# Attention scores in 32x64 column tiles, a reversed second token tile, last products per expert, and a new order of calls, in a fused attention and expert block

## The reference

```
xn = layernorm(x)
out = x + attn(xn) + ffn(xn)

attn: q, k, v = split(xn @ w_qkv.T);  att = softmax(q k.T / sqrt(128))
      y = einsum('bqk,bvd->bqd', att, v) @ w_fc.T + b_fc    # k and v sum apart
      layernorm(xn + y) * gamma + beta
ffn:  h = rms(xn);  16 heads of 8:  q = rms(h wq), k = rms(h wk), v = h wv
      a = softmax(causal(q k.T / sqrt(8))) v;  x1 = xn + (a @ wo.T, first 32 columns 0)
      xf = rms(x1);  weights = top 2 of 4 of softmax(xf @ gate.T), normalised
      moe = w0 o0 + w1 o1 + w2 o2 + w3 o3   # o0: one gelu, o1: silu gate, o2: three gelus, o3: two
      x1 + (moe, first 32 columns 0)
```

## Time and profile before

| | |
|---|---|
| median of three runs | 224.91 us |
| the profiled execution | 224.7 us |
| its span | 223.0 us |
| TensorE busy | 203.4 us (91%) |
| ScalarE busy | 167.6 us (75%) |
| VectorE busy | 137.7 us (62%) |
| GpSimd busy | 106.7 us (48%) |
| granted TensorE clock, mean | 0.991 |

### The profile page before, as it was taken

The page is one execution under the profiler, slowest core; times in us unless marked ns, Lnnn a source line. Parts: engine busy times, 40 slices in busy tenths (PEclk is TensorE's granted clock), DMA queues, the critical chain, the costliest instruction groups (busy, mean ns, idle before and its releaser), DMA issues.

```text
span 223.0 us, 6031 instructions
## 1 busy us (share of the span) xinstructions
PE 203.4 (91%) x2158; PEld 149.8 (67%) x2158; DVE 137.7 (62%) x529; ACT 167.6 (75%) x287; POOL 106.7 (48%) x190
## 2 busy tenths in 40 slices
PE   7888689999999999999999787999999999999872
PEld 6655455568787678676888464578776887678661
DVE  4389938769563526598992476393587555637604
ACT  6457867899999997956689846779789997944530
POOL 7974788973831153147722369425630168010330
PEclk9999999999999999999999999699999999999999
DMA  5950000000000000000000000000000000000001
GB/s 152 296 188 3 3 0 4 0 3 1 0 3 26 0 3 26 0 0 6 0 25 3 26 0 3 1 3 1 3 24 3 1 3 24 3 0 3 24 1 31
DMA packets 5393, 5.00 MB, mean 22 GB/s; under 512 B 498, under 2 KB 4850, under 8 KB 5362
## 3 DMA queue, kind: packets, MB, share of 16 engines
q1 hardware_dynamic: 5216, 4.59, 6.6%
q10 hardware_dynamic: 146, 0.00, 0.0%
HBM read 3.54 MB, written 1.05 MB: 21 GB/s over the span
## 4 chain that ended last, share of the span: by engine, by line
PE 50%; ACT 16%; issue 12%; DVE 12%; POOL 8%; POOLq 0%; ACTq 0%; DVEq 0%
PE even_ps L366 7%; PE scores_ps L252 6%; PE odd_ps L339 5%; PE even_ps L339 5%; PE a_ps L277 5%; ACT probs L742 4%; PE even_ps L398 4%; PE odd_ps L398 3%; PE odd_ps L382 3%; PE odd_ps L192 3%; PE a_ps L222 3%; POOL probs L574 2%; ACT L796 2%; DVE acc L1247 2%; PE a_ps L281 2%
## 5 line engine op out<-in xcount | busy, mean ns | idle before, releaser
L574 POOL TENSOR_SCALAR_AFFINE_SELECT probs<-probs 128x1024 f32<-128x1024 f32 x32 | 35.0, 1094 | 48.6 <-ACT probs L742 48.4
L742 ACT ACTIVATE probs<-scores_ps 128x1536 f32<-128x1536 f32 x32 | 46.4, 1451 | 12.8 <-PE scores_ps L252 12.4
L252 PE MATMUL scores_ps<-qT,kT 32*128 32x128 f32 (+1 forms) x512 | 29.9, 347 | 2.9 <-ACT probs L742 2.7
L252 PEld LDWEIGHTS scores_ps<-qT,kT 32*128 32x128 f32 x512 | 23.5, 184 | 11.9 <-issue 9.5
L366 PE MATMUL even_ps<-l_h,mid 128*128 128x256 f32 x128 | 30.7, 383 | 0.2 <-DVE e_s L1041 0.2
L366 PEld LDWEIGHTS even_ps<-l_h,mid 128*128 128x128 f32 x128 | 23.8, 190 | 4.6 <-ACT l_h L796 0.9
L339 PE MATMUL odd_ps<-xfT,up 128*128 128x256 f32 x80 | 22.9, 401 | 0.8 <-ACT u_h L796 0.8
L277 PE MATMUL a_ps<-probs,v_aug 128*32 128x256 f32 x256 | 20.7, 395 | 1.9 <-ACT kT L848 0.5
L796 ACT ACTIVATE l_h<-even_ps 128x512 f32<-128x512 f32 x24 | 14.3, 597 | 10.0 <-PE even_ps L366 8.3
L796 ACT ACT_TABLE_LOAD x16 | 20.5, 1283 | 1.0 <-PE odd_ps L339 0.3
L1247 DVE SCALAR_TENSOR_TENSOR acc<-even_ps,wts,acc 128x96 f32<-128x96 f32 x32 | 10.1, 317 | 17.4 <-issue 9.9
(11 more groups left out here) (151 smaller groups left out, 435.0 us busy)
## 6 DMA issues: line engine op xcount, KB each, us to landing
x_sb<-in_x SPq DMA_DIRECT2D x8, 128.0 KB, 5.5
out<-acc SPq DMA_DIRECT2D x8, 128.0 KB, 1.8
mid<-in_mid SPq DMA_DIRECT2D x1, 640.0 KB, 7.4
up<-in_up SPq DMA_DIRECT2D x1, 578.0 KB, 6.4
downs<-in_down SPq DMA_DIRECT2D x1, 512.0 KB, 8.3
first<-in_first SPq DMA_DIRECT2D x1, 320.0 KB, 3.9
proj<-in_proj SPq DMA_DIRECT2D x1, 192.0 KB, 2.8
row<-in_rows SPq DMA_DIRECT2D x1, 192.0 KB, 4.8
```

The source lines that it names most:

```text
L252: ins = T.matmul(ps, kT[p][rows, g, kt * P:(kt + 1) * P], qT[p][rows, kt * P:SEQ], start=kt == 0, stop=kt == 1 and not searching, tile_pos ...
L574: nc.gpsimd.affine_select(out=own, in_=own, compare_op=ALU.is_ge, fill=0.0, base=0, pattern=[[0, LANES * TILES], [1, P]], channel_multipli ...
L742: nc.scalar.activation(probs[g][:, :, 0:SEQ + P], scores_ps[:, :, 0:SEQ + P], ACT.Exp).then_inc(s["exp_done"], 1)
```

## The change

- `scores`: all groups but the first use array tiles of 32 rows by 64 columns, so a group has 16 matmuls. Tokens of the second tile are stored in reversed order (the input and the output are turned outside of the kernel). Then the first 64 keys of the first tile are needed by all 256 queries, the next 64 by the last 192; of the second tile's keys the first 64 are needed by 64 queries and the next 64 by 128. What is left out keeps old numbers, which the mask sets to 0.
- `mask`: two selections over 128x512 a group, with opposite signs, in place of one.
- The last batch's `down` becomes four calls `last_down(e)`, one for an expert, in the order 0, 1, 3, 2, that write to `scores_ps`; each waits for its own hidden layer alone. VectorE adds each product when it is there, and each token tile is stored by itself.
- Every engine's list of calls has a new order. TensorE's changes the form of its array tiles 124 times instead of 135 (in the branch that runs), ScalarE's holds 26 table loads instead of 34, and 8 calls of `keep_busy`'s matmul are left of 13.

```diff
+HIDDEN_FILL = ("E0", "E1B", "L3", "U3")
+LAST_ORDER = (0, 1, 3, 2)
...
+                whole = searching or (n == 0 and g == 0)
                 for kt in range(TILES):
-                    for lane in range(LANES):
-                        rows = slice(32 * lane, 32 * lane + 32)
-                        ps = scores_ps[:, lane, 0:SEQ] if kt == 0 else scores_ps[:, lane, SEQ:SEQ + P]
-                        ins = T.matmul(ps, kT[p][rows, g, kt * P:(kt + 1) * P], qT[p][rows, kt * P:SEQ],
-                                       start=kt == 0, stop=kt == 1 and not searching, tile_position=(32 * lane, 0))
+                    for half in range(1 if whole else 2):
+                        part = slice(0, P) if whole else COLUMN_TILES[half]
+                        keys = slice(kt * P + part.start, kt * P + part.stop)
+                        seen = slice(part.start, SEQ) if kt == 0 else slice(P, P + part.stop)
+                        at_col = (SEQ if kt else part.start) if not whole else kt * SEQ
+                        for lane in range(LANES):
+                            rows = slice(32 * lane, 32 * lane + 32)
+                            ins = T.matmul(scores_ps[part, lane, at_col:at_col + seen.stop - seen.start],
+                                           kT[p][rows, g, keys], qT[p][rows, seen], start=kt == 0,
+                                           stop=kt == 1 and not searching, tile_position=(32 * lane, part.start))
...
+            def last_down(e):
+
+                n = BATCHES - 1
+                pe.wait_ge(s["exp_done"], GROUPS * BATCHES)
+                pe.wait_ge(read_sem(HIDDEN_FILL[e]), at[HIDDEN_FILL[e], n] + 1)
+                for j in range(TILES):
+                    for ci in range(HC):
+                        for rows in COLUMN_TILES:
+                            tokens = slice(j * P + rows.start, j * P + rows.stop)
+                            ins = T.matmul(scores_ps[rows, e, j * KEPT:(j + 1) * KEPT], hidden[e][n % 2][:, ci, tokens],
+                                           downs[:, e, ci, MASKED:], start=(ci == 0), stop=(ci == HC - 1),
+                                           tile_position=(0, rows.start))
+                ins.then_inc(s["last_full"], 1)
...
-                keep_busy(4); fold_weights(); x_turn(0); keep_busy(1); qkv_project(0, 0); x_turn(1); qkv_project(0, 1)
...
-                e3_up_layer(7); fc_row(7); l1_layer(7); e1_second(7); l2_layer(7); e0_up(7); l3_layer(7); down(7, 0)
-                down(7, 1)
+                keep_busy(1); x_turn(0); keep_busy(1); qkv_project(0, 0); fold_weights(); x_turn(1); qkv_project(0, 1)
...
+                l2_layer(7); e1_second(7); l3_layer(7); e3_up_layer(7); last_down(0); last_down(1); last_down(3)
+                last_down(2)
...
+            def store_last():
+                for j in range(TILES):
+                    sp.wait_ge(s["last_summed"], j + 1)
+                    sp.dma_start(rows_of(out, BATCHES - 1)[:, j, :], acc[BATCHES - 1][:, j, :]).then_inc(s["out_done"], 16)
...
             def mask(n, g):
 
                 pool.wait_ge(s["exp_done"], GROUPS * n + g + 1)
-                own = probs[g][:].rearrange("p l (n q) -> p (l n) q", q=SEQ)[:, :, 0:P]
-                nc.gpsimd.affine_select(out=own, in_=own, compare_op=ALU.is_ge, fill=0.0, base=0,
-                                        pattern=[[0, LANES * TILES], [1, P]], channel_multiplier=-1
-                                        ).then_inc(s["masked"], 1)
+                for kt, sign in enumerate((1, -1)):
+                    own = probs[g][:, :, kt * SEQ:kt * SEQ + P]
+                    ins = nc.gpsimd.affine_select(out=own, in_=own, compare_op=ALU.is_ge, fill=0.0, base=0,
+                                                  pattern=[[0, LANES], [sign, P]], channel_multiplier=-sign)
+                ins.then_inc(s["masked"], 1)
...
-            search_constants(); ln_variance(0); ln_pow(0); h_square(0); ln_variance(1); h_mean(0); ln_pow(1); h_eps(0)
-            h_square(1); h_pow(0); x1_start(0); h_mean(1); x1_start(1); h_eps(1); biased(0); h_pow(1); biased(1)
...
+            ln_variance(0); ln_pow(0); h_square(0); h_mean(0); h_eps(0); h_pow(0); ln_variance(1); ln_pow(1)
+            h_square(1); h_mean(1); biased(0); x1_start(0); h_eps(1); biased(1); h_pow(1); search_constants()
...
+            def last_down(j, e):
+
+                n, place = BATCHES - 1, LAST_ORDER.index(e)
+                dve.wait_ge(s["last_full"], place + 1)
+                if place == 0:
+                    dve.wait_ge(s["acc_ready"], n + 1)
+                    need("weights", n)
+                else:
+                    need(("last", j, LAST_ORDER[place - 1]), n)
+                kept = acc[n][:, j, MASKED:]
+                ins = V.scalar_tensor_tensor(out=kept, in0=scores_ps[:, e, j * KEPT:(j + 1) * KEPT],
+                                             scalar=wts[n % 2][:, j, e:e + 1], in1=kept, op0=ALU.mult, op1=ALU.add)
+                if place < EXPERTS - 1:
+                    then(ins, ("last", j, e), n)
+                else:
+                    ins.then_inc(s["last_summed"], 1)
...
+    def second_tile_turned(a):
+        tiles = _np.asarray(a).reshape(-1, 2, P, P)
+        return _np.stack([tiles[:, 0], tiles[:, 1, ::-1]], axis=1).reshape(-1, 2 * P, P)
...
-        "x": inputs["L0_attn_x"],
+        "x": second_tile_turned(inputs["L0_attn_x"]),
```

More of the change, by code:

```diff
@@ L261, in scores @@
                     for lane in range(LANES):
-                        own = scores_ps[:, lane, :].rearrange("p (n q) -> p n q", q=SEQ)[:, :, 0:P]
-                        ins = T.matmul(own, ident_bf[:], later_keys[:].unsqueeze(1).to_broadcast([P, TILES, P]),
-                                       start=False, stop=True)
+                        for kt, later in enumerate((later_keys, later_keys_q)):
+                            ins = T.matmul(scores_ps[:, lane, kt * SEQ:kt * SEQ + P], ident_bf[:], later[:], start=False,
+                                           stop=kt == TILES - 1)
                 ins.then_inc(s["scores_full"], 1)
@@ L389, in down @@
                 ps = claim(fill, n)
-                for done in ("E0", "E1B", "L3", "U3"):
+                for done in HIDDEN_FILL:
                     pe.wait_ge(read_sem(done), at[done, n] + 1)
@@ new lines, in batches @@
+                weigh_v(2, 0); gate(1); down(0, 0); down(0, 1); scores(2, 3); q0_project(3); l1_layer(1)
+                weigh_v(2, 1); e0_up(1); a0_scores(3, 0); l2_layer(1); e3_in(1); weigh_v(2, 2); weigh_v(2, 3)
+                e1_first(1); qk_turn(3); e1_second(1); wo_project(2); find_maxima(3); scores(3, 0); l3_layer(1)
+                e3_up_layer(1); a0_scores(3, 1); qkv_project(4, 0); scores(3, 1); down(1, 0); down(1, 1); xf_turn(2)
+                scores(3, 2); gate(2); l1_layer(2); fc_row(3); e3_in(2); scores(3, 3); weigh_v(3, 0); weigh_v(3, 1)
@@ new lines, in batches @@
+                l2_layer(2); e0_up(2); x_turn(5); weigh_v(3, 2); weigh_v(3, 3); e1_first(2); e1_second(2)
+                qkv_project(4, 1); wo_project(3); l3_layer(2); e3_up_layer(2); qkv_project(5, 0); q0_project(4)
+                down(2, 0); down(2, 1); xf_turn(3); qkv_project(5, 1); l1_layer(3); qk_turn(4); e3_in(3); e1_first(3)
+                e3_up_layer(3); gate(3); find_maxima(4); scores(4, 0); e1_second(3); l2_layer(3); e0_up(3)
+                scores(4, 1); qk_turn(5); l3_layer(3); a0_scores(4, 0); down(3, 0); down(3, 1); scores(4, 2)
@@ new lines, in batches @@
+                e3_up_layer(4); e1_first(4); gate(4); qk_turn(6); e1_second(4); xf_turn(5); l3_layer(4); e3_in(5)
+                a0_scores(6, 0); find_maxima(6); scores(6, 0); down(4, 0); gate(5); down(4, 1); scores(6, 1)
+                a0_scores(6, 1); qk_turn(7); e1_first(5); scores(6, 2); e3_up_layer(5); fc_row(6); l1_layer(5)
+                q0_project(7); scores(6, 3); a0_scores(7, 0); weigh_v(6, 0); weigh_v(6, 1); a0_scores(7, 1)
+                find_maxima(7); scores(7, 0); weigh_v(6, 2); weigh_v(6, 3); l2_layer(5); e1_second(5); wo_project(6)
@@ new lines, in batches @@
+                scores(7, 1); fc_row(7); l3_layer(5); weigh_v(7, 0); e0_up(5); xf_turn(6); scores(7, 2); weigh_v(7, 1)
+                down(5, 0); down(5, 1); scores(7, 3); gate(6); l1_layer(6); weigh_v(7, 2); e3_in(6); weigh_v(7, 3)
+                e1_first(6); e0_up(6); wo_project(7); l2_layer(6); e3_up_layer(6); l3_layer(6); xf_turn(7)
+                e1_second(6); l1_layer(7); e3_in(7); gate(7); down(6, 0); down(6, 1); e1_first(7); e0_up(7)
+                l2_layer(7); e1_second(7); l3_layer(7); e3_up_layer(7); last_down(0); last_down(1); last_down(3)
@@ L1345, in batches @@
[L1345 to L1349 removed]
+                ln_normalise(0); ln_statistics(1); ln_moments(1); scale_projection(); ln_normalise(1); head_scales()
```

304 lines of the change are left out of this document (142 added, 162 removed).

## The result

The changed kernel takes **214.49 us**, the median of four runs (213.70 to 216.29), against 224.55 (223.94 to 224.93) for the kernel before on the same chip: a ratio of 0.9566 with a 95% interval from 0.9497 to 0.9634, 10.1 us faster. The profiled execution is the longest of the four: it took 216.29 us with a span of 214.1. Two of the others kept TensorE's granted clock at 1.0 throughout and took 213.70 and 214.04 us; why this one didn't is part of what follows. Runs over 1.5% above the fastest of their kernel are left out of the ratios, which concerns three of the twelve runs of one experiment (e10).

The account below looks back on a forecast made before the run. TensorE's calls were taken to bound 140 of 223 us, chains of waits the rest. Scores -4.8, forms -1.4, masks +0.6, start -2.5, middle -1.0, end -1.9 sum to -11.0: 224.7 to 213.7 us, range 207 to 221.5.

Parts of the forecast that it names:

- scores: 31 of 32 score groups: each 0.706 us instead of 0.86 through column halves running side by side, 4.8 us less.
- masks: GpSimd's two selections a group instead of one: 0.6 us more, from three places where TensorE waits for a mask.
- start: Start of the kernel: earlier root and shorter VectorE chain 3.2 us, less 0.7 for fewer dummies: 2.5 us less.
- end: Batch 7's down products cover the last gelu and two products follow instead of four: 1.9 us less.
- forms, tables, middle: Fewer array-form changes 1.4 us less, fewer ScalarE table loads nothing, shorter wait and clock drop mid-kernel 1.0 less.
- I count all 31: Scores: the full 0.154 us saving counted in each of 31 groups, 4.8 us, even where TensorE isn't the bound.
- a half waits for the other half's pass: Rival for the score groups: matmuls start in written order, 384 columns as now, 1.5 us saved, 217.0 us; chance 0.17.
- The root at 4.0 us: Start, GpSimd: with mask constants moved behind both batches' roots, the first root starts at about 4.0 us, 1.9 earlier.
- the first xn at 4.8: Sign at the start: batch 0's xn, which follows the first root, at 4.8 us; 6.71 before.
- The first scores about 3 us before now: Sign at the start: the first score group begins about 3 us earlier than in the kernel before.
- A granted clock under 1.0 in the first 40 us: Sign that the prediction would be wrong: TensorE's granted clock below 1.0 in the first 40 us.
- I took a third of 3.1: Middle: of TensorE's 1.30 us wait behind batch 5's scores and 1.8 us of lowered clock, 1.0 us comes back.

Follow-up runs that it names:

- e10: Kernel before with the mask constants moved behind the roots of batches 0 and 1 in GpSimd's order: ratio 1.0093, 2.1 us slower.
- e1: Changed kernel with every score group on whole 32x128 tiles again: 217.3 us, ratio 0.9664.
- e2: Kernel before with only the new score tiles, reversed second tile and two masks; old orders and old end: 222.75 us, ratio 0.9936.
- e6: Kernel before with its one mask a group split into two of 128x512: 224.01 us, ratio 0.9987.
- e5: Changed kernel with the old end (two calls of down products, eight products on VectorE, one store): 216.51 us, ratio 0.964.
- e8: Changed kernel unaltered, run again for its own spread: 214.05 us, ratio 0.9532.
- e3: Changed kernel without the reversal of the second token tile, halves streaming 384 and 256 columns: 214.83 us, ratio 0.9581.
- e9: e4 with four more dummy matmuls where TensorE waits for batch 0's normalised heads: 214.19 us, ratio 0.9532.
- e7: Changed kernel with more dummy matmuls at the start, ahead of the first turn and of batch 1's projection: 214.88 us, ratio 0.9577.
- e11: e9 with two added dummy matmuls instead of four: 213.87 us, ratio 0.9534.
- e4: Changed kernel with batch 1's root moved ahead of the biased copies and the residual's start in GpSimd's order: 215.22 us, ratio 0.9567.

## Why the prediction was right, and where its steps were not

213.7 us were predicted and 214.49 measured. The score group got shorter by the mechanism named; that the total fits so well is in part luck, since the terms were not all of the right size:

| term | predicted | measured | by |
|---|---|---|---|
| scores | -4.8 | -2.2 to -3.0 in the new order (-2.3 by the traces), -1.4 in the old | e1, e2 |
| masks | +0.6 | -0.9 to +0.3, in the old order | e6 |
| start | -2.5 | -1.6, -2.2 or -3.8 (first scores) | profiles of the changed kernel, e5, e8 |
| end | -1.9 | -1.6 by the traces, -2.5 by the medians | e5, e8 |
| forms, tables, middle | -2.4 | not separated | |

**Scores.** The group came out nearly as worked out (0.706, read 0.70 in the chain; by its hold on TensorE, 0.865 and 0.729, it gained 0.136 us and not 0.154), and e3 shows the reason, two queues of which the longer counts. What was mis-sized is the sentence "I count all 31". A group's gain is a gain only until the next call that waits for another engine. From 40 to 120 and 140 to 200 us I had called TensorE the bound on account of its busy share, but there ScalarE's gelus and VectorE's products finish only just ahead of the calls that need them, and 0.136 us is more than that margin at some of them: of 4.2 us about 1.9 were given back. The Trainium skill (TensorE: Matmul & The Clock Gate, "The mechanism") has matmuls in strict program order; if that meant that a half waits for the other half's pass, e3 and the changed kernel would have had equal groups. They have 0.81 and 0.70, and matmuls of 128 columns start ahead of those of 64 that are written before them, so the measurement decides.

**The start.** The root at 4.0 us (4.08) and the first xn at 4.8 (4.83) came as said. "The first scores about 3 us before now" came as 1.57 in one profile and 3.81 in the other; of the ends that I gave, 0.8 and 3.2, the first lies inside and the second outside. I hadn't seen that GpSimd's new order puts two copies that need the rows ahead of batch 1's root, so that the start follows the landing of a transfer. "A granted clock under 1.0 in the first 40 us" was named as a sign of being wrong; it happened, behind that wait. That the fewer dummies bring it is not shown: e8 and e9 have as few of them ahead of the first turn, and no drop in their profiles. But the fewer dummies are not without a price: in e5's profile, with the same calls at the start, TensorE's calls still run at half speed up to about 10.7 us, and the first scores come at 18.20 us with no drop behind them, 1.6 us later than in e8, where I had taken 0.7. e10 shows that the term's 1.9 us for the earlier root was no property of that edit: alone it costs 2.1 us. In the new TensorE order batch 2 isn't needed so early; what the move is worth there no run shows alone, only that the first scores come 1.6 to 3.8 us sooner with all changes of the start together.

**The middle.** The wait of the earlier trace rows is 0.59 us instead of 1.30:

```profile
138.23 0.41 PE L189 MATMUL b_ps<-ident,xf 128*128 128x128 f32 x2 [0.59 <-DVE xf L1241]
```

The stage's idle time fell by 1.21 us, no wait of over 2 us came ahead of batch 4's second norm, and the clock stayed up. What the drop had cost is 1.2 us, not 1.8, and only in some runs: of 58 runs of the kernel before beside the experiments, 27 with a clock of 0.994 or more took 223.61 to 224.20 us and 31 with 0.992 or less 224.65 to 225.72 us, 223.9 and 225.1 in the mean; in both profiles with such a clock (before and e6) it is this drop. Nor does the wait alone bring the drop: e2's profile, in the old order, has it and keeps a clock of 1.00 over the 6 us behind.

```profile
139.56 0.44 PE L189 MATMUL b_ps<-ident,xf 128*128 128x128 f32 x2 [1.32 <-ACT a_exp L777]
```

I took a third of 3.1; the rows speak for more, but no run has this part alone.

**Forms and tables.** ScalarE is 9.6 us less busy, as said. Whether any of that came back, and what the 11 fewer changes of form gave, wasn't tried. By subtraction from the first pair of profiles, 8.9 us of span less 2.3 for the scores, 1.6 for the start and 1.6 for the end leaves 3.4 us for forms, tables, masks and the middle, 1.8 predicted; this is a remainder, and the drop that only the kernel before has in the middle of this pair is in it.

**The end.** The four calls had no wait; e5 has one of 0.86 us and four products behind the last matmul, 1.6 us in all.

So the total was right by two errors of opposite sign: about 2 us too much for the scores and, by that remainder, 1.6 too little for forms, tables, masks and the middle.

## What to carry to other kernels

A shorter call pays only up to the margin of the next wait: multiply the saving by the calls, then look, call by call, at how long the partner engine's result had been ready, not at the busy share. A move in one engine's order has no price of its own (here 2.1 us lost in one order, and no delay seen in the other); ask which call of the others stands first behind the place where it lands. And where a kernel's time varies with something at its start, compare a stretch behind the cause (here from the first exponential on), which agreed to 0.05 us in five profiles with the same calls there (190.58 to 190.63 us; the first, e7, e8, e9 and e11) whose spans differ by 2.3.

## What the runs showed of the hardware

- In two-pass f32 matmuls on 32x64 tiles the two column halves of a strip run beside each other. With 384 columns in the longest, the group held TensorE for 0.809 us, with 320 for 0.729; on 32x128 tiles with 384 it was 0.865. 64 columns fewer gave 0.080 us, 1.25 ns each, less than the 1.68 that I had used.
- One and the same kernel ran with and without a drop of the clock to its lower level in its first 20 us. The drops seen there stand behind TensorE's waits of 1.85 us (changed kernel), 1.93 (e1) and 1.57 (e4); the profiles without one had waits of 1.26 us (e5) or less ahead of the first scores, and with e4's wait filled by dummies all eleven runs had a clock of 0.997 to 1.0. But a wait doesn't settle it: in the middle of the old order the clock fell behind a wait of 1.30 us (before) and kept its level behind one of 1.32 (e2).
- When TensorE's opening calls reach full speed differs between runs too: the same first projection of 384 columns took 0.88 us in e8 and 1.57 in e5, which started alike.
- The landing of one transfer, that of the rows, differed by over 1 us between two profiles of the same kernel (6.0 and 4.9 us from issue to landing; the first copy that needs it at 9.43 and at 8.27 us). With the drop of the clock that followed in the one of them, the first scores moved by 2.2 us. In e1's profile it took 6.2 us, and there too TensorE waited and the clock fell; in the six other profiles that have the changed kernel's start or a variant of it (e3, e4, e5, e7, e9, e11) it took 4.5 to 5.5.
